# Attention of a hybrid layer: two rings of PSUM banks, exponentials of two heads, score tiles in groups of four

## The reference

```python
q = jnp.einsum('bse,hde->bhsd', x, Wq) + bq[None, :, None, :]
k = jnp.einsum('bse,hde->bhsd', x, Wk) + bk[None, :, None, :]
v = jnp.einsum('bse,hde->bhsd', x, Wv) + bv[None, :, None, :]
scores = jnp.einsum('bhsd,bhtd->bhst', q, k) / jnp.sqrt(jnp.asarray(D, x.dtype))
w = jax.nn.softmax(scores, axis=-1)
o = jnp.einsum('bhst,bhtd->bhsd', w, v)
o = jnp.transpose(o, (0, 2, 1, 3)).reshape(B, S, H * D)
return o @ Wo.T + bo          # E = 128, H = 16, D = 8
```

## Time and profile before

| | us |
|---|---|
| median of 3 runs | 1502.6 |
| lowest, highest | 1468.61, 1514.92 |
| profiled execution, its own time | 1479.49 |
| its span | 1477.7 |
| TensorE busy / VectorE / ScalarE / GpSimd | 91% / 77% / 63% / 5% |
| mean granted TensorE clock | 0.913 |

### The profile page before, as it was taken

The page is one execution under the profiler, slowest core; times in us unless marked ns, Lnnn a source line. Parts: engine busy times, 40 slices in busy tenths (PEclk is TensorE's granted clock), DMA queues, the critical chain, the costliest instruction groups (busy, mean ns, idle before and its releaser), DMA issues.

```text
span 1477.7 us, 21707 instructions
## 1 busy us (share of the span) xinstructions
PE 1343.2 (91%) x7955; PEld 743.3 (50%) x7955; DVE 1136.6 (77%) x2645; ACT 932.9 (63%) x1746; POOL 74.2 (5%) x72
## 2 busy tenths in 40 slices
PE   2779999886999999999999999999999888999999
PEld 1468898772323333333333333324333222898898
DVE  7587787769767787898878888878888850787786
ACT  1146566451756678777768767768877766556555
POOL 1032000010000000000000000000000000000000
PEclk8789999995857899998989999989999966999999
DMA  4100000000000000000000000000000000000000
GB/s 168 32 1 1 1 1 1 1 1 0 1 1 0 1 0 1 1 1 1 1 1 1 1 1 0 1 0 1 1 1 1 1 1 1 8 8 8 16 8 16
DMA packets 6120, 10.83 MB, mean 7 GB/s; under 512 B 1907, under 2 KB 3574, under 8 KB 5878
## 3 DMA queue, kind: packets, MB, share of 16 engines
q1 hardware_dynamic: 6014, 9.45, 1.9%
HBM read 7.28 MB, written 2.10 MB: 6 GB/s over the span
## 4 chain that ended last, share of the span: by engine, by line
PE 72%; DVE 16%; ACT 8%; issue 3%; DMA 0%; SPq 0%; DVEq 0%; ACTq 0%
PE six L1203 17%; PE six L1026 15%; PE acc L1271 14%; DVE mxp L826 9%; ACT PB L504 5%; PE six L1015 4%; PE six L1017 4%; PE six L1016 4%; PE six L1131 4%; ACT tr L477 2%; PE misc L1015 1%; PE misc L1138 1%; PE misc L1144 1%; PE misc L925 1%; PE misc L1017 1%
## 5 line engine op out<-in xcount | busy, mean ns | idle before, releaser
L504 ACT ACTIVATE PB<-six 128x512 f32<-128x512 f32 x1024 | 556.0, 599 | 247.8 <-PE six L1203 236.9
L826 DVE TENSOR_REDUCE mxp<-six 128x2 f32<-128x1024 f32 x512 | 600.0, 1217 | 102.4 <-PE six L1131 101.3
L1203 PE MATMUL six<-Q,K 32*128 32x512 f32 x1024 | 360.8, 519 | 38.2 <-ACT PB L504 35.6
L1203 PEld LDWEIGHTS six<-Q,K 32*128 32x128 f32 x1024 | 147.8, 198 | 387.3 <-ACT PB L504 345.2
L1271 PE MATMUL acc<-PB,Vg 128*32 128x512 f32 x2048 | 308.6, 678 | 9.8 <-ACT PB L504 6.3
L1026 PEld LDWEIGHTS six<-w2s,PB 128*128 128x128 f32 x2048 | 247.4, 192 | 9.4
L1026 PE MATMUL six<-w2s,PB 128*128 128x128 f32 x2048 | 251.1, 276 | 0.0
L428 ACT ACTIVATE PB<-six 128x512 f32<-128x512 f32 x256 | 151.6, 599 | 144.4 <-PE six L1017 124.1
L1131 PE MATMUL six<-K,Q 32*128 32x512 f32 x1024 | 191.8, 529 | 25.2 <-DVE mxp L826 24.6
L716 DVE SCALAR_TENSOR_TENSOR x<-six,wexp,x 128x128 f32<-128x128 f32 x512 | 143.8, 343 | 49.0 <-PE six L1026 47.3
L761 DVE TENSOR_TENSOR PB<-PB 128x512 f32<-128x512 f32 x128 | 98.8, 772 | 50.8 <-ACT PB L428 48.2
(11 more groups left out here) (192 smaller groups left out, 940.3 us busy)
## 6 DMA issues: line engine op xcount, KB each, us to landing
x<-in_x SPq DMA_DIRECT2D x4, 512.0 KB, 5.7
SC<-in_w_om SPq DMA_DIRECT2D x1, 2048.0 KB, 14.2
out<-x SPq DMA_DIRECT2D x8, 256.0 KB, 2.0
VH<-in_w SPq DMA_DIRECT2D x1, 1024.0 KB, 9.5
Vg<-in_wqs SPq DMA_DIRECT2D x1, 256.0 KB, 7.6
Vg<-in_wks SPq DMA_DIRECT2D x1, 256.0 KB, 5.9
cst<-in_cst SPq DMA_DIRECT2D x1, 81.5 KB, 3.3
nwb<-in_nw SPq DMA_DIRECT2D x1, 64.0 KB
```

Source lines behind the costliest of these rows:

```text
L504: act.activation(PB[:, k % 2, j, :], scores, ACT.Exp).then_inc(G_("exp_done"), 1)
L826: dve.reduce_max(mxp[:, th, t, 2 * i:2 * i + 2], sm[:, i, :].rearrange("p (a n) -> p a n", a=2), AX.X).then_inc(G_("max_done"), 1)
L1203: pe.matmul(sl[:, j % banks, :], K[rows, g, t * P:(t + 1) * P], Q[rows, g, u * BLK:(u + 1) * BLK], start=True, stop=True).then_inc(G_("s2_ ...
```

## The change

PSUM is divided anew. Banks 0 to 3 are two pairs (`pairs`), a ring for what ScalarE reads; banks 4, 5 and `misc` are a ring of three (`max_banks`) for what VectorE reads; `acc` stays. `bank_order` lists in program order what passes through either ring, tiles and side tasks alike, and gives each its number; item n waits until item n-2 (ScalarE's ring) or n-3 (VectorE's ring) has been taken. Four semaphores count that (`act_filled`, `act_taken`, `max_filled`, `max_taken`).

- Second pass: the tiles of two heads fill a pair, and one exponential reads 128 x 1024.
- First pass: each head's tile has a bank of its own, and one `reduce_max` reads 128 x 512. The heads are rotated by two.
- TensorE's order in a step: scores of heads 0 and 1 with maxima tiles of heads 2 and 3; scores of heads 2 and 3 with maxima tiles of heads 0 and 1; values' products of the step before; a task for ScalarE; a task for VectorE. The last group has the same order without maxima.
- Side tasks that ScalarE reads (projections, values, output rows, turned layer norm) go through the pairs, those that VectorE reads (turned maxima, turned outputs, product with Wo) through the ring of three. The step in which each is done is as before, but in the first group the values and the four projections come in steps 0 to 5. VectorE does its task after the maxima of the step, where before it did it ahead of them.
- Splitting of queries and keys: ScalarE's second copy now also applies the mask (a scale and a bias by partition, `mbias`), into one of two buffers `tr`, and GpSimd adds the two copies (`split_out`) in place of VectorE.

```diff
+    for s in range(STEP0, STEP1):
+        for i in range(2 if s >= 0 else 0):
+            AR["exp", s, i] = len(AR)
+        if act_task(s):
+            AR[act_task(s)] = len(AR)
+        for i in range(HG if s < STEP1 - STEPS else 0):
+            DR["max", s, i] = len(DR)
+        if max_task(s):
+            DR[max_task(s)] = len(DR)
...
-        se = six[:, 0:2]
-        sl = six[:, 0:HG]
-        sm = six[:, 2:6].rearrange("p (r a) n -> p r (a n)", a=2)
+        pairs = six[:, 0:4].rearrange("p (r a) n -> p r (a n)", a=2)
...
+        max_banks = (six[:, 4, :], six[:, 5, :], misc[:])
...
+            def split_out(G, task):
...
+                pl.tensor_tensor(dst, qf[:, task % 2, :], tr[:, task % 2, :].bitcast(F32), ALU.add
+                                 ).then_inc(G_("qk_split"), 1)
...
+            for s in range(STEP0, STEP1):
+                for i in range(2 if s >= 0 else 0):
+                    scores = taken_pair("exp", s, i)
+                    if i == 0 and s >= 2:
+                        act.wait_ge(G_("pv_done"), s - 1)
+                    act.activation(PB[:, s % 2, 2 * i:2 * i + 2, :].rearrange("p a n -> p (a n)"), scores, ACT.Exp
+                                   ).then_inc(G_("act_taken"), 1)
+                    if i == 1 and s % 8 == 0 and s:
+                        acc_out(s // 8 - 1)
+                side_task(s)
...
+            def maxima(s):
+
+                t, th = s % STEPS // 2, s % 2
+                for i in range(HG):
+                    j = (i + 2) % HG
+                    dve.reduce_max(mxp[:, th, t, j:j + 1], taken_bank("max", s, i), AX.X).then_inc(G_("max_taken"), 1)
...
+                if s < STEP1 - STEPS:
+                    maxima(s)
+                side_task(s)
+                if kk in (7, 15) and s < STEP1 - STEPS:
+                    minus_max(s, kk // 8)
...
+            def free_pair(*key):
+                n = AR[key]
+                if n >= ACT_SLOTS:
+                    pe.wait_ge(G_("act_taken"), n - ACT_SLOTS + 1)
+                return pairs[:, n % ACT_SLOTS, :]
+
+            def free_bank(*key):
+                n = DR[key]
+                if n >= MAX_BANKS:
+                    pe.wait_ge(G_("max_taken"), n - MAX_BANKS + 1)
+                return max_banks[n % MAX_BANKS]
...
             for s in range(STEP0, STEP1):
                 for i in range(2):
+                    if s >= 0:
+                        scores(s, i)
+                    if s < STEP1 - STEPS:
+                        first_pass(s, 2 * i)
+                        first_pass(s, 2 * i + 1)
+                if s > 0:
+                    times_values(s - 1)
+                fill_for_act(s)
+                fill_for_max(s)
+            times_values(STEP1 - 1)
```

More of the change, by code:

```diff
@@ L1118, in values @@
[L1118 removed]
+                g, block = G % NG, 2 * (G // NG) + task // 2
+                return three(bank, wh[:, g, :], wl[:, g, :], (block % 4) * BLK)
+            def values(r, bank):
                 for i in range(TPK):
[L1120 removed]
+                    ins = pe.matmul(bank[:, i * P:(i + 1) * P], hf[:, r, i * P:(i + 1) * P], wvT[:],
                                     start=True, stop=True)
[L1122 removed]
@@ L1124, in first_pass @@
-            def first_pass(count, g, kk, i):
-                t, th = kk // 2, kk % 2
-                if not (isinstance(count, int) and count == 0 and kk == 0):
-                    pe.wait_ge(G_("max_done"), count + 2 * kk + i - 1)
-                for a in range(2):
-                    rows = slice(RB * (2 * i + a), RB * (2 * i + a + 1))
-                    ins = pe.matmul(sm[:, i, a * BLK:(a + 1) * BLK], Q[rows, g, t * P:(t + 1) * P],
-                                    K[rows, g, th * BLK:(th + 1) * BLK], start=True, stop=True)
-                ins.then_inc(G_("s1_done"), 1)
@@ new lines, in scores @@
+            def scores(s, i):
+                G, kk = divmod(s, STEPS)
+                u, t = divmod(kk, TPB)
+                slot = free_pair("exp", s, i)
+                if i == 0 and t == 0:
+                    pe.wait_ge(*max_taken("turn", G, u))
+                for c in range(2):
+                    rows = slice(RB * (2 * i + c), RB * (2 * i + c + 1))
+                    ins = pe.matmul(slot[:, c * BLK:(c + 1) * BLK], K[rows, G % NG, t * P:(t + 1) * P],
+                                    Q[rows, G % NG, u * BLK:(u + 1) * BLK], start=True, stop=True)
+                ins.then_inc(G_("act_filled"), 1)
@@ new lines, in times_values @@
+            def times_values(s):
+                G, kk = divmod(s, STEPS)
+                t = kk % TPB
+                pe.wait_ge(*act_taken("exp", s, 1))
+                if kk == 0:
+                    pe.wait_ge(G_("vg_ready"), G + 1)
+                if t == 0 and s:
+                    pe.wait_ge(G_("acc_stored"), s // 8)
+                for j in range(HG):
+                    ins = pe.matmul(acc[RB * j:RB * (j + 1), :], Vg[:, G % 2, t, j, :], PB[:, s % 2, j, :],
+                                    start=(t == 0), stop=(t == TPB - 1))
+                ins.then_inc(G_("pv_done"), 1)
```

602 lines of the change are left out of this document (274 added, 328 removed).

## The result

| | before | after |
|---|---|---|
| median of 20 runs each, us | 1488.94 | 1497.67 |
| lowest, highest | 1468.61, 1514.92 | 1481.66, 1519.72 |
| profiled execution, its span | 1479.49, 1477.7 | 1511.16, 1509.4 |
| mean granted clock of that execution | 0.913 | 0.904 |
| TensorE / VectorE / ScalarE / GpSimd busy | 91 / 77 / 63 / 5% | 86 / 75 / 59 / 10% |

The changed kernel is slower, by 1.0% in the ratio (1.0098 [1.006, 1.0137]) and by 0.6% in the medians: clear of noise, but less than 2%. The forecast was 1482 and 1.4% faster.

A forecast was written before the change was run, and what follows sets the result against it. The kernel was taken to be bound by a loop of latencies through two PSUM banks. From the profiled 1479.5 us, -12 (groups) +25 (extras) +9 (first group) -19 (last group) -1 (clock) gave 1482; eight-in-ten range 1436 to 1532.

The forecast's parts named there:

- The anchor: Whole kernel: the summed 1482 us was held against the 1502.6 median of the runs shown, giving -1.4%.
- The loop: Attention steps: TensorE waits on VectorE's maxima through the ring of three; 2.72 us without a task, 51.4 a group.
- Rival D: Attention groups: VectorE's sum is the bound and the ring hides the products; 1416 to 1440 us, chance 0.10.
- rival C: Attention steps: matmuls on four row groups don't run together, 0.3 us more in every step; 1554 us, chance 0.06.
- What fifteen such groups save: Fifteen groups with both passes: 51.4 us each against 52.2, 0.8 less, 12 us in all.
- The values: Value tasks of the next batch in a batch's last group: no term in the sum, so 0 us.
- The extras: Layer norm (6 blocks, 31 us) and output rows (3 batches, 11) now delay the loop; less 17 before, net +25.
- First and last group: First group, maxima alone: +9 us from tasks ahead of the tiles; last group, no maxima: 57 becomes 38, -19.
- The clock: TensorE's clock in the fifteen groups: layer norm's steps cost 27 us against about 28 before, -1.
- Denser steps: Steps without a task get denser, so clock falls outside layer norm's steps should go; part of the -1.
- Rival A: Attention: the clock stays up since denser steps carry TensorE over, six falls don't happen; 1455 us, chance 0.22.
- rival B: Attention: half clock persists, 27 us for each further low group; three give 1562 us, chance 0.12.

The follow-up runs named there:

- e14: Changed kernel without layer norm's statistics and root inside the attention, GpSimd's output-bias addition moved to the next group's start: 1457.3 us, ratio 0.987 to the kernel before.
- e11: Changed kernel with two exponentials of 128x512 for each pair of banks instead of one of 128x1024: 1501.4 us, ratio 1.018 to the kernel before.
- e2: Kernel before with the statistics and inverse root of the next batch's layer norm left out inside the attention: 1451.2 us, ratio 0.981.
- e10: e3 with GpSimd's addition of the output bias moved from a group's end to the start of the next: 1428.4 us, ratio 0.971 to the kernel before.
- e6: Changed kernel with the values' products between the two groups of four instead of behind both: 1469.1 us, ratio 0.990 to the kernel before.
- e7: e3 and e6 together, on the changed kernel: median 1491.5 us, from 1441 to 1534, ratio 0.978 to the kernel before.
- e9: e3 with the values' products between the groups of four only in the four steps that follow a projection: 1455.3 us, ratio 0.984 to the kernel before.
- e12: e9 and e10 together, on the changed kernel: 1443.1 us, ratio 0.979 to the kernel before.
- e15: Kernel before with layer norm moved into projection steps 4 to 7 and the bias addition to a later group's start: 1480.5 us, ratio 0.9998.
- e3: Changed kernel with layer norm's VectorE work moved from steps 8, 10, 12 to projection steps 4 to 7: 1449.1 us, ratio 0.982 to the kernel before.
- e16: The kernel of e10 run once more, beside e15 on the same chip: 1429.7 us, ratio 0.971 to the kernel before.

## Why the prediction failed

Where two numbers stand as "2.74 for 2.72", the first is measured and the second is the forecast's.

**The anchor** (its last step, "I hold 1482 against the median"). The sum said 2 us slower than the profiled execution, and I turned that into 1.4% faster by setting it against a median of three. The median of 20 runs is 1488.9, 13.7 lower. Of the 16 us between the sum (1481.5) and 1497.7, 9.4 are the profiled execution's distance from its median and 6.7 the change itself (+8.7 where the sum had +2). A change of +2 with its own uncertainty should have been carried to either time as +2. This step alone turned the sign; the sum itself had the right one, too small.

**The loop** held: 2.74 for 2.72, minus-maximum step 3.05 for 3.2, steps with turned maxima 3.45 for 3.54 and with turned outputs 3.35 for 3.43, projection steps 15.6 for 15.2, group 51.5 for 51.4. Rival D fell (maxima wait for PE: 94 + 51 us on the page) and rival C (no step is 0.3 longer).

**What fifteen such groups save** was over-counted: -9 for -12. Full-clock halves of after are 28.0 + 23.5, of before 27.0 + 24.9: 0.4 less and not 0.8. (The 52.2 I compared with is the group that holds the values of the next batch.) Fourteen of these make -6. The group without projections I should have summed apart: 51.4 less 4 x 1.08 is 47.1; measured 46.3, against 49.8 at full clock (2 x 24.9) and 52.1 in the profile: -3.5.

**The values** were left out of the sum. They are two tasks through the pairs in the last group of a batch: 25.6 against a half of 23.5 after, 25.3 against 24.9 before, so 1.7 in each of three batches, +5 for 0.

**The extras**: +26 for +25. Output rows cost 3.0 in their second half (26.5 against 23.5) and 0.6 in the first (28.6 against 28.0), against 0.7 before: +9. (The recorded parts of layer norm, 1.16 + 2.2 + 1.4, make 4.8 and not the 4.6 that I wrote; that is 1 us in all.) Layer norm's halves are nowhere wholly at full clock in after; e14's half with norm and transposes alone is 25.1, 1.6 over 23.5, and statistics and root last 1.5 and 2.1 in the trace, together 5.2 for 5.2. Before it was 2.4 in the one half at full clock (28.0 against 25.6): 6 x 2.8 = +17. That it lies wholly on the path is right at full clock; in a stretch at half clock much of it is covered (above), so +17 may be too much.

**First and last group**: +6 for +9, -19 for -19. e11 shows why the last one came: with two exponentials it is still 36.5 of 53.1, so the order and the banks made it, not the wide exponential. But most of the 19 is clock. The two last groups:

```profile
1201.29:1254.40 53.11, 46.05 (x202) 11.90 (x203) 6.03 (x30) 33.36 (x65) 1.27 (x1) 0.60 0.00 1
1252.07:1285.93 33.86, 30.91 (x203) 9.42 (x204) 6.03 (x30) 30.62 (x36) 1.28 (x1) 1.00 0.00 1
```

Before ran it at 0.60, which is 42 us of half clock, after at 1.00. In e2 the last 8 steps ran at 0.99 in the old order and took 18.4, against 17.1 in the new; at full clock throughout the gain would be about 3 (an estimate: twice 18.4 less 33.9). I had 57 and 38, so either level was 4 too high and the difference came out by luck.

All of these terms sum to -9 + 5 + 26 + 6 - 19 = +9, where the forecast had +3. That the two lines at 103 us are 10 apart looks like a second proof and isn't one: of the kernel before's 103 us the line puts some 42 into the last group, whose cost the -19 already holds. With 42 us more for before, as in the terms, the lines stand at 1446 ± 2 (at 145) and 1443 ± 2 (at 103), 3 the other way.

**The clock** (-1). Between the profiles the halves with layer norm and those behind them look like a loss of 54 us. Over all runs the clock costs both kernels the same, but the forecast had put the last group's share into its -19, and its -1 was for the fifteen groups alone. There, past the 103 us that e10 has outside them and past before's 42, the means leave 154 us of half clock after and 131 before, which cost 54 and 40 by the slopes: about +14 for -1 (an estimate). So this is the term of the sum that was mis-sized. I had expected falls outside layer norm's steps to go and half clock to stay as long in all; instead the waits for layer norm, 1.6 to 2.3 us where the profile of before has at most 0.7 in these steps, were each followed by a fall, and half clock lasted up to 52 us behind them.

With +14 the terms make +23 where the medians differ by 8.7, so the account doesn't close. Which term is too large isn't shown; the weakest is the +17 for layer norm, which rests on one half of the kernel before and on full clock in after.

"Denser steps" are what e6, e7, e9 and e12 have, and they had more half clock than e10 (e6 and e7 more than after too). Rival A's condition, that the falls don't happen, came true only where the stalls were removed, in e10. That half clock lasts, as rival B has it, is seen in e7. The Trainium skill's rule on cycling through PSUM banks (TensorE: Matmul & The Clock Gate, "A second HAM failure mode: psum-queue depth-cycling"), which I had put beside B, isn't borne out as a matter of the rings: e10 cycles through the same two rings and has no half clock there.

**What stays open.** What lets the clock of the kernel before fall isn't known: without statistics and root it has 168 us of half clock in the mean instead of 276 (e2), but in e15's attention PE waits 0.7 us at most for an exponential, and its clock falls all the same. In e10 a wait for the copies of a projection lasts up to 1.4 us without a fall, and of equal waits of 1.25 us in e3 four were followed by a fall and two were not, so the length of one wait alone doesn't decide. How much of the 8.7 us is the loop and how much the clock is open by some 12 us, as said above. And why half clock, once there, ends after 10 us in one place and after 50 in another was not isolated.

## What to carry to other kernels

Where time follows the clock this closely (11 us for each 0.01 of it in the changed kernel), look at clock and span of many runs before reading two profiles against each other, and carry a summed difference over as a difference, to whichever time. In a loop closed over two engines each small operation of the one that is waited for is on the path: find the steps in which another engine binds and put that work there, all of it, since one such stall left over was enough to lose 20 us. Shortening the loop first can lose by the clock what it gains.

## What the runs showed of the hardware

- A VectorE operation of 128 x 16 with both inputs in SBUF took 0.67 us instead of 0.17 while a 1.28 us GpSimd addition ran.
- Waits of PE of 1.25 us for one bank were followed by half clock in 4 of 6 places (e3), waits of 0.75 in the same steps, with the same work around them, in none of 12 (e10, e16); waits of 1.13 in 4 of 6 (e14).
- Half clock lasted 86 us with PE counted busy 93% of it, in matmuls of 32 rows or 32 columns (e7). A us of it cost 0.31 us of span in the kernel before and 0.35 in the changed one.
- One exponential over 128 x 1024 in PSUM took 1.025 us, two over 512 0.599 each; a maximum over 512 columns took 0.682, over 1,024 1.217.
